# Attention in a macaron block: the spread key norms signalled, and subtracted from the scores, in two groups of columns

## What is computed

```python
s   = einsum('id,jd->ij', qr, conj(kr)).real        # rotated queries and keys
qn  = (q.real**2 + q.imag**2).sum(-1)
kn  = (k.real**2 + k.imag**2).sum(-1)
E   = exp(clip(-mu * |t_i - t_j|, -30, 0))          # the decay
V   = sigma_sq / (2*mu) * (1 - E*E) + eta_sq + gamma_sq
maha = maximum(qn[:, None] + E*E * kn[None, :] - 2*E*s, 0) / V
logits = coef * log1p(maha / nu) - 0.5 * 64 * log(V)   # causal mask, softmax
y   = softmax(logits) @ v   ->   projected by Wo, added to x
```

## Time and profile before

| | us |
|---|---|
| median of 3 runs (1732.48 to 1736.56) | 1736.48 |
| the profiled execution, its own time | 1734.65 |
| its span | 1732.9 |
| attention, first to last start of line 1511 | 263.9 to 1504.1 |

### The profile page before, as it was taken

How to read it: one execution, slowest core, us unless ns; L and a number is a source line. 1 busy time by engine, 2 the same in 40 slices (tenths; PEclk the granted TensorE clock), 3 DMA queues, 4 the chain that set the end, 5 groups by cost and what they waited for, 6 DMA issues and landing times. The chain is left out here.

```text
span 1732.9 us, 30643 instructions
## 1 busy us (share of the span) xinstructions
PE 1654.3 (95%) x9664; PEld 1333.6 (77%) x9664; DVE 1472.9 (85%) x3350; ACT 1478.9 (85%) x2939; POOL 985.7 (57%) x841
## 2 busy tenths in 40 slices
PE   5999988999999999999999999999999999899998
PEld 4787766878887887788788878877887887677876
DVE  6878877899889988988998999899889889977675
ACT  6677767999999999999999999999989999766755
POOL 3554555556556655656655666566556555345565
PEclk9999998999999999999999999999999999999999
DMA  6000032232213222222322222222222322100000
GB/s 173 1 1 1 1 101 65 50 77 54 72 50 77 65 56 71 62 65 50 77 64 63 65 62 71 56 65 62 65 66 61 77 50 58 30 1 13 13 7 19
DMA packets 42993, 92.29 MB, mean 53 GB/s; under 512 B 7376, under 2 KB 19280, under 8 KB 42832
## 3 DMA queue, kind: packets, MB, share of 16 engines
q1 hardware_dynamic: 42832, 90.33, 20.6%
HBM read 17.95 MB, written 5.24 MB: 13 GB/s over the span
## 5 line engine op out<-in xcount | busy, mean ns | idle before, releaser
L1445 POOL TENSOR_TENSOR early<-early 128x1024 f32<-128x1024 f32 x128 | 305.3, 2385 | 487.9 <-PE pS L1133 253.7
L646 POOL TENSOR_TENSOR hid_lo_d<-hid_d,hid_hi_d 128x512 fp32r<-128x512 f32 x176 | 231.4, 1315 | 219.1 <-ACT hid_hi_d L557 212.5
L1133 PE MATMUL pS<-early 128*128 128x128 f32 (+3 forms) x1024 | 299.9, 436 | 2.8 <-POOL early L1445 2.8
L1328 ACT ACTIVATE early<-early,qnorm 128x128 f32<-128x128 f32 (+3 forms) x512 | 246.3, 554 | 64.7 <-DVE early L1515 64.7
L1311 ACT ACTIVATE early<-early,nmax 128x128 f32<-128x128 f32 (+3 forms) x512 | 281.2, 560 | 16.2 <-DVE nmax L1502 15.7
L1511 DVE SCALAR_TENSOR_TENSOR pS<-pS,ek 128x1280 f32<-128x1280 f32 x128 | 191.8, 1498 | 109.3 <-PE pS L1133 109.1
L1133 PEld LDWEIGHTS pS<-early 128*128 128x128 f32 x1024 | 165.7, 192 | 99.0 <-issue 62.6
L1453 POOL TENSOR_TENSOR ek<-early 128x128 f32<-128x128 f32 (+3 forms) x256 | 216.1, 877 | 15.7 <-ACT early L1319 15.7
L1453 POOL TENSOR_TENSOR ek<-decay,early 128x128 f32<-128x128 f32 (+3 forms) x256 | 215.0, 873 | 2.2 <-ACT early L1319 2.1
L1148 PEld LDWEIGHTS pV<-ones,early 128*128 128x128 f32 x1016 | 134.4, 193 | 61.6 <-issue 61.6
L1173 PE MATMUL pS<-ident,early 128*128 128x128 f32 x1280 | 164.2, 274 | 7.0 <-DVE early L1515 5.7
(11 more groups left out here) (386 smaller groups left out, 3954.8 us busy)
## 6 DMA issues: line engine op xcount, KB each, us to landing
early<-early SPq DMA_DIRECT2D x256, 256.0 KB, 3.6
early<-trig_d SPq DMA_DIRECT2D x64, 64.0 KB, 2.0
trig_d<-early SPq DMA_DIRECT2D x3, 1024.0 KB, 6.9
early<-in_w SPq DMA_DIRECT2D x3, 704.0 KB, 8.7
x_sb<-in_x SPq DMA_DIRECT2D x4, 512.0 KB, 8.4
early<-in_wqk SPq DMA_DIRECT2D x16, 128.0 KB, 3.5
cos<-trig_d SPq DMA_DIRECT2D x32, 64.0 KB, 2.1
sin<-trig_d SPq DMA_DIRECT2D x32, 64.0 KB, 2.0
```

Source lines behind the costliest of these rows:

```text
L646: g.tensor_tensor(hid_lo[:, par], hid[:, par], hid_hi[:, par].bitcast(F32), ALU.subtract).then_inc(lo_done, 1)
L1133: last = pe.matmul(s.pS[:, span(I)], rot[:, I * P:(I + 1) * P], rot[:, N:N + (I + 1) * P], start=True, stop=True)
L1328: last = a.activation(u[:, span(I)], u[:, span(I)], ACT.Relu, bias=qnorm[:, r % 2, I:I + 1])
L1445: g.tensor_tensor(rot[:], by_cos[:], crossed[:], ALU.add).then_inc(S["rot_done"], 1)
```

## The change

The subtraction is done for each group by itself, right ahead of the group's product with the decay. ek_done and w_done now count two for each pair. GpSimd signals ek after row tiles 0 and 2 and again after 3 and 1, and waits ahead of each group for w_done of that group of the pair before. The wait for zred_done (the end of `peaks`) moves ahead of the first subtraction. The arithmetic and the number of elements are unchanged.

```diff
             def key_norms(i, r):
-                wait(a, S["ek_done"], n)
+                wait(a, S["ek_done"], 2 * n)
...
             def spread(i, r):
...
-                wait(g, S["w_done"], n)
-                for I in ORDER:
-                    last = g.tensor_tensor(ek[:, span(I)], decay[par][:, span(I)], knorm[:, 0:(I + 1) * P], ALU.mult)
-                last.then_inc(S["ek_done"], 1)
+                for k, (_, pieces) in enumerate(HALVES):
+                    wait(g, S["w_done"], 2 * (n - 1) + k + 1)
+                    for I in pieces:
+                        last = g.tensor_tensor(ek[:, span(I)], decay[par][:, span(I)], knorm[:, 0:(I + 1) * P], ALU.mult)
+                    last.then_inc(S["ek_done"], 1)
...
             def distances(i, r):
                 wait(v, S["s_done"], n + 1)
-                wait(v, S["ek_done"], n + 1)
-                v.scalar_tensor_tensor(s.pS[:, 0:SW], s.pS[:, 0:SW], -2.0, ek[:], ALU.mult, ALU.add).then_inc(S["w_done"], 1)
-                wait(v, S["w_done"], n + 1)
                 wait(v, S["zred_done"], 2 * n)
-                for half, _ in HALVES:
+                for k, (half, _) in enumerate(HALVES):
+                    wait(v, S["ek_done"], 2 * n + k + 1)
+                    v.scalar_tensor_tensor(s.pS[:, half], s.pS[:, half], -2.0, ek[:, half], ALU.mult,
+                                           ALU.add).then_inc(S["w_done"], 1)
+                    wait(v, S["w_done"], 2 * n + k + 1)
                     v.tensor_tensor(u[:, half], s.pS[:, half], decay[par][:, half], ALU.mult).then_inc(S["t_done"], 1)
```

## The result

The changed kernel takes 1754.95 us (median of 5 runs, 1751.32 to 1756.66) against 1736.31 us before (5 runs). The ratio is 1.011, with a 95% interval of 1.0095 to 1.0125: slower by 1.1%.

A forecast was written before the change was run, and what follows sets the result against it. Odd heads were taken as bound by a VectorE-TensorE loop, even heads by TensorE. 1.60 us per odd and 0.84 per even head, times eight, gave 19.5 us on 1734.65: 1754 us, range 1742 to 1760.

The forecast's parts named there:

- The bound: Odd heads: VectorE from scores to `accumulate` and TensorE from `weigh` to scores form one loop; even heads: TensorE sets the pace.
- The split: Subtraction in pS: pieces of 0.73 and 0.98 us, together 0.21 us more than one; second product ends 0.24 us later.
- The first rival: A dependence on VectorE is free: 0.13 us extra or less, 8.1 us in all, 1742.7 us; chance 0.13.
- The moved wait: Waiting for the end of `peaks` delays the subtraction behind `build_front` by 0.11 us, once in each odd head; elsewhere hidden.
- A met wait: Rival: the second subtraction's already met ek_done wait costs another 0.11 us; 30 us in all, 1765 us; chance 0.07.
- ScalarE took no gain: Rival: ScalarE uses its 0.66 us idle ahead of `clamp`; 16 entries save 10.6 us, 1724 us; chance 0.05.
- nothing would change: Rival: odd heads' loop isn't closed and the margins swallow the rest; 1735 to 1740 us; chance 0.05.
- The margin of the even heads: Second product has 0.13 us to spare before `turn`'s fifth weight load; 0.11 us too late, five times, costs 0.55 us.
- The margin of the fifth load: In even heads, `turn`'s fifth weight load starts 0.13 us after the second product would let it.
- the build stretch: Three of a head's eight intervals, around the builds, where ScalarE's table work is last; together 0.29 us added per head.
- ScalarE: Third piece of `clamp` waits for the second product, so `clamp` ends 0.29 us later, reaching TensorE only entering build stretches.
- The sum: Per 16 pairs, 1.60 us for the odd head and 0.84 for the even, together 2.44; times eight, 19.5 us.

The follow-up runs named there:

- fillers: Kernel before plus a 128-column VectorE instruction in each of 128 steps, ahead of `accumulate` (1767.69 us) or behind it (1752.07 us).
- the swap: Kernel before with `accumulate` ahead of the query norms in odd heads: 1731.43 us beside 1734.88 (0.9987).
- split_only: Changed kernel with the split subtraction but GpSimd signalling and waiting once per pair, and no ek_done wait at the second subtraction: 1756.05 us (1.0113).
- curve: Kernel before with a VectorE filler between the two products of a pair, growing from none to 384 columns over the heads: 1820.83 us, one execution.

## Why the prediction held

**The bound.** Right, and shown. In odd heads the way from the subtraction to `accumulate` is in a closed loop with `weigh` and `scores`: the interval takes fillers of 0.29 to 1.25 us to the hundredth, the swap gives its 0.13 us back, and the split's 0.20 us come out as 9.22. In even heads TensorE sets the pace and the second product matters beyond a margin.

**The split.** 0.24 us forecast, 0.20 measured. The fixed part was mis-sized: I drew a line through the 128- and the 1280-column instruction of the earlier trace rows for 0.21 us, but the pieces took 699 and 955 ns, 0.156 us more together than the one. The gap behind a dependence was right at 0.03 us (878.41 + 0.70 to 879.14), and the second product took 0.01 us more than before. The result lies between this and the bound of 0.13 us for free dependences, nearer to the forecast.

**The first rival**, free dependences, had 1742.7 us. The lateness of 0.20 us and the 9.22 us speak against it here. The Trainium skill (VectorE: DVE Perf Modes, section The DRAIN you can't avoid) reports that a semaphore after each of eight copies cost nothing extra; for this chain of dependent instructions the trace disagrees, with a product 0.03 us behind the end of its subtraction (878.41 + 0.70 to 879.14). The moved wait, 0.19 us from the start of the last read to the subtraction where it had been 0, speaks against it once more.

**The other rivals.** A met wait costs nothing: the second subtraction, which waits for ek_done, starts 0.08 us ahead of the end of the first product (879.75 against 879.14 + 0.69), and `split_only`, without that wait, has the same 9.22 us. ScalarE took no gain, since its third piece waits for the second product. That nothing would change fell with the closed loop: the plain odd intervals grew by the 0.20 us.

**The margin of the even heads.** 0.13 us forecast, 0.17 measured (`curve`). Together with the smaller lateness this leaves 0.02 us a pair and not 0.11. The margin of the fifth load was right at 0.13 us. I had taken a late weight load as a late matmul in full; 0.05 to 0.06 us of the load's lateness never reached the matmuls. With that, the smaller lateness and the build stretch below, the even heads cost 0.23 us each, not 0.84.

**The moved wait.** 0.11 us forecast, 0.19 measured. I had counted the read of the last result, 0.08 us, and a gap of 0.03; the gap is 0.11 us (840.67 + 0.08 to 840.86). Why it is wider than the one behind a subtraction isn't shown. The interval behind the front build, for which 0.24 + 0.11 were forecast, grew by 0.22 us in the mean, since in three heads it had been longer before. The wait also acts in the last head, which I had left out.

**ScalarE.** Direction right: `clamp` ends later, and its idle time moved between its second and third piece. On entry to the build stretch of even heads I had 0.29 us; the long intervals grew by 0.07 and fell by 0.01, and with 0.02 for the one ahead the stretch cost 0.09 us. `curve` agrees: its long intervals grew by no more with delays of 0.33 to 0.71 us. For odd heads the stretch's three intervals grew by 0.33 us in the mean of the seven heads, near the 0.29, but from 0.21 to 0.63; in four of them it is the 0.20 to 0.25 us of the loop and little more. So the 0.29 us on entry aren't confirmed.

**The sum.** 19.5 us were forecast for the attention. The seven odd heads before the last gave 1.49 us each against 1.60, and the last 2.6, so the odd heads gave 13.1 us against 12.8. The even heads gave 0.23 against 0.84, and the first took 0.5 us less; in sum 1.2 against 6.7. So the sum was 5.3 us too high in the attention (14.2), all of it in the even heads. In the profiled execution the 2.3 us behind the attention, at half clock, were no term of mine. The medians differ by 18.6 us, 2 more than the profiled spans: the changed kernel's profiled execution was the fastest of its five. The mean granted clock was 0.987 to 0.992 of full in those five, and 0.992 or more in most of the kernel before. So 1754 against 1754.95 is in part luck: the even heads' terms were too large, and what lies behind the attention and in the scatter was missing.

## What to carry to other kernels

An engine that idles in every round can still be on the path: look for what its last instruction releases, and whether the work behind that brings back the engine's own next input. Splitting an instruction for an earlier release pays only if somebody waits for the first part; the second part always comes later, here by 0.20 us, and its reader inherits that. To find which stretch of an engine matters, put the same filler inside and outside of the suspected loop and compare intervals, not totals.

## What the runs showed of the hardware that I had not expected

- A VectorE instruction that takes both inputs from SBUF waited for the GpSimd instruction in flight: the filler of 128 columns took 275 to 1347 ns in one kernel, and in 233 of 256 cases in two kernels it ended 0.143 to 0.156 us behind the end of that GpSimd instruction. The subtractions, with one input in PSUM and one in SBUF, repeated to 1% beside it (1484 to 1500 ns).
- Behind the attention TensorE was granted half of full clock for 6.8 or 13.7 us in the profiles of the five split kernels and of `curve`, and full clock there in the other eight. This went with 2.3 to 5.0 us of the time, and with 2.3 of the 16.6 us of this change.
- A wait for the instruction just ahead isn't free on VectorE: the next one started 0.19 us behind the start of a read that it had overlapped in full before. A wait for ek_done, met long before, cost nothing: the overlap of 0.08 us stayed.
